# A decoder layer on one core: fourteen products of zeros leave TensorE's queue, and all five written orders are made anew

## What is computed

```python
x = x + attention(layernorm(x), Wqkv, Wo)        # 16 heads of 16, rotary positions, causal
x = x + cross_attention(layernorm(x), ctx, mask) # one head of 256, softmax over 256 context rows
x = x + ffn(layernorm(x), ...)                   # 8 experts of 176, the best 2 of each token, and a shared one of 352
```

## Time and profile before

| what | us |
|---|---|
| three runs | 269.67, 270.72, 271.45 |
| their median | 270.72 |
| span of the profiled execution | 271.7 |
| busy in it: PE, DVE, ACT, POOL | 259.4, 170.0, 174.8, 122.4 |
| mean granted TensorE clock | 0.994 |

### The profile page before, as it was taken

One profiled execution on the slowest core, in us unless ns is written; L12 is line 12 of the kernel. 1 busy time (PEld: TensorE's weight loads), 2 busy tenths in 40 slices (PEclk: granted clock), 3 DMA queues, 4 the chain that ended last, 5 costly groups with the idle time before them and its releaser, 6 DMA issues.

```text
span 271.7 us, 4900 instructions
## 1 busy us (share of the span) xinstructions
PE 259.4 (95%) x1805; PEld 210.2 (77%) x1810; DVE 170.0 (63%) x361; ACT 174.8 (64%) x292; POOL 122.4 (45%) x133
## 2 busy tenths in 40 slices
...
PEclk9997999999999999999999999999999999999999
...
DMA packets 11879, 17.08 MB, mean 63 GB/s; under 512 B 1904, under 2 KB 8272, under 8 KB 11856
## 3 DMA queue, kind: packets, MB, share of 16 engines
...
## 4 chain that ended last, share of the span: by engine, by line
PE 71%; POOL 8%; DMA 6%; DVE 6%; issue 4%; ACT 3%; SPq 2%; DVEq 0%; ACTq 0%
PE bank L789 26%; PE bank L898 13%; PE bank L802 11%; PE bank L951 4%; DMA res<-x 4%; POOL prob_lo L419 3%; DMA w_raw<-w 3%; PE bank L843 3%; PE bank L796 2%; PE bank L829 2%; PE bank L867 2%; PE bank L822 2%; PE bank L847 2%; POOL w_lo L426 1%; PE bank L824 1%
## 5 line engine op out<-in xcount | busy, mean ns | idle before, releaser
L419 POOL TENSOR_TENSOR prob_lo<-prob,prob_hi 128x1536 f16<-128x1536 f32 x16 | 49.9, 3120 | 14.9 <-ACT prob_hi L542 14.8
L789 PE MATMUL bank<-x_hi,w_hi 128*128 128x512 f32 x112 | 45.5, 406 | 0.0
L789 PE MATMUL bank<-x_hi,w_lo 128*128 128x512 f32 x112 | 44.2, 395 | 0.0
L789 PE MATMUL bank<-x_lo,w_hi 128*128 128x512 f32 x112 | 44.1, 393 | 0.0
L615 DVE TENSOR_REDUCE negm<-bank 128x2 f32<-128x512 f32 (+1 forms) x48 | 31.6, 685 | 8.6 <-PE bank L824 6.6
L771 DVE TENSOR_TENSOR h_lo<-h_c,h_hi 128x512 fp32r<-128x512 f32 x28 | 23.6, 845 | 21.0 <-ACT h_hi L581 20.8
L581 ACT CAST h_hi<-h_c 128x512 fp32r<-128x512 f32 x28 | 17.3, 617 | 24.6 <-DVE h_c L766 17.1
L757 DVE TENSOR_TENSOR h_c<-bank,h_s 128x512 f32<-128x512 f32 x28 | 19.3, 688 | 21.9 <-PE bank L789 18.3
L898 PE MATMUL bank<-w_hi,h_hi 128*128 128x256 f32 x112 | 32.9, 294 | 0.1
L575 ACT ACTIVATE h_s<-bank 128x512 f32<-128x512 f32 x28 | 16.7, 596 | 24.7 <-PE bank L789 24.7
L898 PE MATMUL bank<-w_hi,h_lo 128*128 128x256 f32 x112 | 31.6, 283 | 0.0
(11 more groups left out here) (128 smaller groups left out, 573.3 us busy)
## 6 DMA issues: line engine op xcount, KB each, us to landing
w_raw<-w SPq DMA_DIRECT2D x3, 1792.0 KB, 8.2
...
```

The lines of the kernel that those rows point to most:

```text
L419: eng.tensor_tensor(prob_lo[:, b % 2], prob[:, b % 2], prob_hi[:, b % 2], ALU.subtract)\
L789: ins = pe.matmul(dst, a(k), c(k), start=(k == 0 and i == 0), stop=(k == kt - 1 and i == 2))
```

## The change

PE's list loses its eight `early` and `late` entries (`early.4`, `.3`, `.1`, `.2`, `.1`, `.1` and twice `late.1`), 14 products of zeros in all, and the branches that issued them go. The sixteen ahead of the list stay. All five lists are written anew from the same steps. No step but those is added or dropped, and no instruction or wait inside a step is changed.

```diff
     "SP": """
-        ln1.0 mt.0 mt.1 mt.2 mt.3 mt.4 ct.0 mt.5 w3.0 ct.1 ro.0 ro.1 cb.0 ct.2 ct.3 y.0 cb.1 y.1
+        ln1.0 mt.0 mt.1 mt.2 mt.3 mt.4 ro.0 ro.1 ct.0 w3.0 mt.5 ct.1 cb.0 ct.2 ct.3 cb.1 y.0 y.1
     "POOL": """
-        ln1.0 ln1.1 qk.0 sh.0 qk.1 sh.1 qk.2 ln1.2 w12.0 qk.3 ln1.3 sh.2 w12.1 sh.3 qk.4 tr.7 h.0 h.1 sh.4 h.2 h.3
-        qk.5 sh.5 h.4 w12.2 ln2.0 w12.3 h.5 h.6 qk.6 sh.6 ln3.0 h.7 qk.7 w12.4 w12.5 sh.7 ln2.1 w12.6 h.8 w12.7 h.9
-        w12.8 h.10 ln3.1 h.11 h.12 h.13 w12.9 w3.0 ln2.2 w3.1 h.14 w3.2 w12.10 w3.3 w3.4 w12.11 ln3.2 h.15 w3.5
+        ln1.0 ln1.1 qk.0 sh.0 qk.1 sh.1 ln1.2 ln1.3 qk.2 sh.2 qk.3 w12.0 tr.7 w12.1 sh.3 qk.4 h.0 h.1 sh.4 h.2 h.3
+        qk.5 sh.5 h.4 w12.2 ln2.0 w12.3 w12.4 h.5 h.6 qk.6 ln3.0 sh.6 qk.7 h.7 sh.7 h.8 ln2.1 w12.5 h.9 h.10 w12.6
+        ln3.1 h.11 w12.7 h.12 w12.8 w3.0 h.13 w3.1 w12.9 ln2.2 h.14 w3.2 w12.10 w12.11 w3.3 ln3.2 h.15 w12.12 w3.4
...
     "ACT": """
-        ln1n.0 xt.0 ln1n.1 v.0 sh.0 xt.1 vm.0 tr.0 tr.1 sh.1 w12.0 w12.1 w12.2 tr.4 tr.5 ln1n.2 sh.2 v.1 w12.3 sh.3
-        xt.2 ln1n.3 mt.0 w12.4 mt.1 vm.1 tr.8 tr.9 s.0 s.1 tr.12 tr.13 s.2 s.3 h.0 w12.5 s.4 s.5 h.1 s.6 s.7 s.8
+        ln1n.0 xt.0 ln1n.1 v.0 sh.0 w12.0 xt.1 vm.0 tr.0 tr.1 sh.1 tr.4 tr.5 sh.2 w12.1 ln1n.2 sh.3 v.1 xt.2 w12.2
+        mt.0 ln1n.3 mt.1 vm.1 tr.8 tr.9 s.0 s.1 tr.12 tr.13 s.2 s.3 h.0 s.4 s.5 h.1 sh.4 s.6 w12.3 s.7 s.8 h.2 s.9
...
-        s.30 s.31 xs.1 s.32 pt.1 h.10 s.33 mt.4 s.34 s.35 h.11 s.36 ln3n.1 s.37 t3.1 s.38 mt.5 vm.3 s.39 s.40 lg.1
-        s.41 up.0 h.12 h.13 ct.1 up.1 w3.0 dn.0 ot.2 s.42 s.43 s.44 dn.1 s.45 w3.1 up.2 ln2n.2 s.46 t2.2 h.14 s.47
-        w12.10 xs.2 up.3 w3.2 pt.2 w3.3 w3.4 up.4 w3.5 dn.2 h.15 w12.11 dn.3 ln3n.2 w3.6 up.5 t3.2 dn.4 w3.7 dn.5
+        pt.1 w12.6 vm.3 s.33 mt.4 s.34 s.35 h.11 ln3n.1 s.36 s.37 t3.1 s.38 w12.7 mt.5 s.39 h.12 s.40 lg.1 s.41 up.0
+        ct.1 w12.8 w3.0 w3.1 h.13 ot.2 up.1 w3.2 dn.0 w12.9 w3.3 s.42 s.43 w12.10 ln2n.2 s.44 s.45 t2.2 s.46 s.47 h.14
+        dn.1 xs.2 up.2 pt.2 up.3 dn.2 w12.11 w3.4 up.4 ln3n.2 h.15 dn.3 up.5 w3.5 dn.4 w3.6 w3.7 t3.2 w12.12 up.6 w3.8
...
     "DVE": """
-        ln1.0 ln1.1 zero.0 qk.0 ln1.2 v.0 ln1.3 qk.1 vm.0 kt.2 kt.3 qk.2 m.0 m.1 m.2 kt.6 kt.7 m.3 qk.3 m.4 m.5 m.6
-        m.7 m.8 m.9 m.10 m.11 v.1 zero.1 vm.1 kt.10 kt.11 qk.4 kt.14 kt.15 m.12 m.13 m.14 m.15 m.16 m.17 m.18 m.19
+        ln1.0 ln1.1 zero.0 qk.0 zero.1 v.0 qk.1 ln1.2 ln1.3 vm.0 kt.2 kt.3 qk.2 m.0 m.1 m.2 kt.6 m.3 kt.7 qk.3 m.4 m.5
+        m.6 m.7 m.8 m.9 m.10 m.11 v.1 vm.1 kt.10 kt.11 qk.4 kt.14 kt.15 m.12 m.13 m.14 m.15 m.16 m.17 pv.0 m.18 m.19
...
-        ln3.1 m.44 m.45 pv.9 m.46 m.47 t3.1 pv.10 lg.1 rk.1 up.0 pv.11 vm.3 on.2 dn.0 up.1 pv.12 wo.2 ln2.2 dn.1
-        pv.13 xs.2 up.2 xc.2 up.3 dn.2 ro.2 ln3.2 dn.3 up.4 pv.14 up.5 dn.4 t3.2 up.6 dn.5 pv.15 lg.2 rk.2 up.7 on.3
+        m.44 m.45 m.46 m.47 t3.1 vm.3 pv.10 lg.1 rk.1 up.0 pv.11 on.2 up.1 wo.2 ln2.2 dn.0 xs.2 pv.12 dn.1 xc.2 pv.13
+        up.2 up.3 dn.2 ro.2 ln3.2 dn.3 up.4 up.5 pv.14 t3.2 dn.4 up.6 lg.2 dn.5 rk.2 up.7 pv.15 on.3 dn.6 up.8 wo.3
...
     "PE": """
-        xt.0 qk.0 v.0 qk.1 xt.1 early.4 tr.0 tr.1 qk.2 tr.2 tr.3 m.0 tr.4 tr.5 m.1 m.2 tr.6 m.3 tr.7 qk.3 m.4
-        m.5 v.1 m.6 m.7 xt.2 m.8 m.9 mt.0 m.10 m.11 early.3 mt.1 tr.8 tr.9 qk.4 tr.10 s.0 tr.11 s.1 tr.12 s.2
-        tr.13 s.3 early.1 tr.14 early.2 tr.15 s.4 early.1 m.12 m.13 s.5 m.14 m.15 s.6 m.16 s.7 m.17 m.18 s.8
-        m.19 s.9 m.20 pv.0 s.10 m.21 m.22 pv.1 m.23 s.11 early.1 mt.2 qk.5 tr.16 tr.17 s.12 pv.2 s.13 tr.18 s.14
+        xt.0 qk.0 v.0 qk.1 xt.1 tr.0 tr.1 qk.2 tr.2 tr.3 m.0 tr.4 m.1 tr.5 m.2 m.3 tr.6 tr.7 qk.3 m.4 m.5 v.1 m.6 m.7
+        xt.2 m.8 m.9 mt.0 m.10 m.11 mt.1 tr.8 tr.9 s.0 qk.4 tr.10 tr.11 s.1 tr.12 s.2 tr.13 s.3 tr.14 tr.15 s.4 s.5
+        m.12 m.13 s.6 m.14 m.15 s.7 m.16 m.17 pv.0 m.18 s.8 m.19 s.9 m.20 m.21 s.10 m.22 m.23 s.11 pv.1 mt.2 qk.5
...
-        s.29 late.1 tr.31 s.30 s.31 m.36 m.37 t2.1 m.38 xs.1 m.39 m.40 s.32 pv.8 m.41 pt.1 m.42 s.33 m.43 ro.1
-        mt.4 s.34 m.44 s.35 pv.9 m.45 s.36 s.37 m.46 m.47 pv.10 t3.1 s.38 mt.5 s.39 late.1 s.40 lg.1 s.41 up.0
-        s.42 pv.11 ct.1 up.1 ot.2 s.43 pv.12 wo.2 s.44 s.45 pv.13 s.46 up.2 s.47 dn.0 t2.2 dn.1 xs.2 up.3 pt.2
+        m.43 ro.1 mt.4 s.34 s.35 m.44 pv.9 m.45 s.36 pv.10 m.46 m.47 s.37 t3.1 s.38 s.39 mt.5 s.40 lg.1 s.41 up.0 s.42
+        pv.11 ct.1 s.43 up.1 ot.2 pv.12 wo.2 up.2 s.44 s.45 dn.0 t2.2 s.46 s.47 xs.2 up.3 pt.2 pv.13 dn.1 ro.2 up.4
...
@@
                 elif part == "dn":
                     down(b)
-                elif part == "early":
-
-                    idle_products(ps_tail, b)
-                elif part == "late":
-
-                    pe.wait_ge(s["rope_ok"], NT * B)
-                    idle_products(ps_qk, b)
```

More of the change, by code:

```diff
@@ L61 @@
-        w12.12 w3.6 ln2.3 w3.7 w3.8 w12.13 w3.9 w3.10 w3.11 w3.12 ln3.3 w3.13
+        ln1.0 ln1.1 qk.0 sh.0 qk.1 sh.1 ln1.2 ln1.3 qk.2 sh.2 qk.3 w12.0 tr.7 w12.1 sh.3 qk.4 h.0 h.1 sh.4 h.2 h.3
+        qk.5 sh.5 h.4 w12.2 ln2.0 w12.3 w12.4 h.5 h.6 qk.6 ln3.0 sh.6 qk.7 h.7 sh.7 h.8 ln2.1 w12.5 h.9 h.10 w12.6
+        ln3.1 h.11 w12.7 h.12 w12.8 w3.0 h.13 w3.1 w12.9 ln2.2 h.14 w3.2 w12.10 w12.11 w3.3 ln3.2 h.15 w12.12 w3.4
+        w3.5 ln2.3 w3.6 w12.13 w3.7 w3.8 w3.9 w3.10 ln3.3 w3.11 w3.12 w3.13
@@ L69 @@
-        s.30 s.31 xs.1 s.32 pt.1 h.10 s.33 mt.4 s.34 s.35 h.11 s.36 ln3n.1 s.37 t3.1 s.38 mt.5 vm.3 s.39 s.40 lg.1
-        s.41 up.0 h.12 h.13 ct.1 up.1 w3.0 dn.0 ot.2 s.42 s.43 s.44 dn.1 s.45 w3.1 up.2 ln2n.2 s.46 t2.2 h.14 s.47
-        w12.10 xs.2 up.3 w3.2 pt.2 w3.3 w3.4 up.4 w3.5 dn.2 h.15 w12.11 dn.3 ln3n.2 w3.6 up.5 t3.2 dn.4 w3.7 dn.5
-        up.6 lg.2 w3.8 up.7 w12.12 w3.9 w3.10 ct.2 dn.6 up.8 dn.7 ot.3 up.9 ln2n.3 dn.8 t2.3 up.10 w12.13 dn.9 xs.3
-        pt.3 dn.10 w3.11 w3.12 up.11 ln3n.3 w3.13 up.12 t3.3 up.13 dn.11 dn.12 lg.3 dn.13 up.14 up.15 dn.14 ct.3
@@ L74 @@
-        dn.15 up.16 dn.16 up.17 dn.17 up.18 dn.18 up.19 dn.19 up.20 dn.20 up.21 dn.21 up.22 up.23 dn.22 dn.23 up.24
-        dn.24 up.25 up.26 dn.25 up.27 dn.26 dn.27
+        ln1n.0 xt.0 ln1n.1 v.0 sh.0 w12.0 xt.1 vm.0 tr.0 tr.1 sh.1 tr.4 tr.5 sh.2 w12.1 ln1n.2 sh.3 v.1 xt.2 w12.2
+        mt.0 ln1n.3 mt.1 vm.1 tr.8 tr.9 s.0 s.1 tr.12 tr.13 s.2 s.3 h.0 s.4 s.5 h.1 sh.4 s.6 w12.3 s.7 s.8 h.2 s.9
+        s.10 s.11 mt.2 h.3 tr.16 s.12 s.13 tr.17 s.14 sh.5 h.4 v.2 ot.0 tr.20 s.15 tr.21 vm.2 s.16 s.17 h.5 s.18
@@ new lines @@
+        ln2n.0 w12.4 s.19 t2.0 s.20 w12.5 xt.3 h.6 xs.0 pt.0 s.21 s.22 sh.6 ln3n.0 s.23 mt.3 t3.0 h.7 tr.24 sh.7 lg.0
+        s.24 tr.25 s.25 s.26 s.27 ct.0 h.8 ot.1 tr.28 s.28 s.29 tr.29 s.30 v.3 s.31 ln2n.1 s.32 t2.1 h.9 h.10 xs.1
+        pt.1 w12.6 vm.3 s.33 mt.4 s.34 s.35 h.11 ln3n.1 s.36 s.37 t3.1 s.38 w12.7 mt.5 s.39 h.12 s.40 lg.1 s.41 up.0
+        ct.1 w12.8 w3.0 w3.1 h.13 ot.2 up.1 w3.2 dn.0 w12.9 w3.3 s.42 s.43 w12.10 ln2n.2 s.44 s.45 t2.2 s.46 s.47 h.14
+        dn.1 xs.2 up.2 pt.2 up.3 dn.2 w12.11 w3.4 up.4 ln3n.2 h.15 dn.3 up.5 w3.5 dn.4 w3.6 w3.7 t3.2 w12.12 up.6 w3.8
@@ L76 @@
+        w3.9 dn.5 lg.2 up.7 w3.10 w3.11 ct.2 up.8 ot.3 dn.6 w3.12 up.9 ln2n.3 w3.13 w12.13 dn.7 t2.3 up.10 dn.8 xs.3
+        dn.9 up.11 pt.3 dn.10 up.12 dn.11 ln3n.3 dn.12 t3.3 up.13 up.14 dn.13 dn.14 lg.3 up.15 up.16 ct.3 dn.15 up.17
+        dn.16 dn.17 up.18 up.19 dn.18 dn.19 up.20 up.21 up.22 dn.20 up.23 dn.21 dn.22 up.24 up.25 dn.23 up.26 dn.24
+        dn.25 up.27 dn.26 dn.27
     """,
     "DVE": """
-        ln1.0 ln1.1 zero.0 qk.0 ln1.2 v.0 ln1.3 qk.1 vm.0 kt.2 kt.3 qk.2 m.0 m.1 m.2 kt.6 kt.7 m.3 qk.3 m.4 m.5 m.6
@@ L79 @@
-        m.7 m.8 m.9 m.10 m.11 v.1 zero.1 vm.1 kt.10 kt.11 qk.4 kt.14 kt.15 m.12 m.13 m.14 m.15 m.16 m.17 m.18 m.19
-        m.20 pv.0 m.21 m.22 m.23 pv.1 qk.5 pv.2 kt.18 pv.3 on.0 kt.19 v.2 wo.0 kt.22 ln2.0 kt.23 vm.2 m.24 m.25 m.26
-        m.27 pv.4 m.28 xs.0 m.29 m.30 qk.6 m.31 pv.5 m.32 xc.0 ro.0 ln3.0 m.33 m.34 m.35 pv.6 qk.7 t3.0 pv.7 lg.0
-        rk.0 on.1 kt.26 kt.27 wo.1 ln2.1 kt.30 kt.31 m.36 m.37 v.3 m.38 xs.1 m.39 m.40 m.41 pv.8 m.42 m.43 xc.1 ro.1
-        ln3.1 m.44 m.45 pv.9 m.46 m.47 t3.1 pv.10 lg.1 rk.1 up.0 pv.11 vm.3 on.2 dn.0 up.1 pv.12 wo.2 ln2.2 dn.1
@@ L84 @@
-        pv.13 xs.2 up.2 xc.2 up.3 dn.2 ro.2 ln3.2 dn.3 up.4 pv.14 up.5 dn.4 t3.2 up.6 dn.5 pv.15 lg.2 rk.2 up.7 on.3
-        dn.6 dn.7 up.8 wo.3 ln2.3 dn.8 up.9 up.10 xs.3 dn.9 dn.10 xc.3 ro.3 ln3.3 up.11 t3.3 up.12 dn.11 dn.12 up.13
-        lg.3 rk.3 up.14 dn.13 dn.14 up.15 dn.15 y.0 up.16 dn.16 up.17 dn.17 up.18 dn.18 up.19 dn.19 up.20 dn.20
-        up.21 dn.21 up.22 dn.22 up.23 dn.23 up.24 dn.24 up.25 dn.25 up.26 up.27 dn.26 dn.27 y.1
+        ln1.0 ln1.1 zero.0 qk.0 zero.1 v.0 qk.1 ln1.2 ln1.3 vm.0 kt.2 kt.3 qk.2 m.0 m.1 m.2 kt.6 m.3 kt.7 qk.3 m.4 m.5
@@ new lines @@
+        m.6 m.7 m.8 m.9 m.10 m.11 v.1 vm.1 kt.10 kt.11 qk.4 kt.14 kt.15 m.12 m.13 m.14 m.15 m.16 m.17 pv.0 m.18 m.19
+        m.20 m.21 m.22 m.23 pv.1 qk.5 pv.2 kt.18 pv.3 on.0 kt.19 v.2 wo.0 kt.22 kt.23 ln2.0 m.24 vm.2 m.25 m.26 m.27
```

(8 more changed lines are left out.)

18 lines of the change are left out of this document (8 added, 10 removed).

## The result

| what | us |
|---|---|
| changed kernel, four runs | 274.88, 276.42, 276.62, 278.41 |
| their median | 276.52 |
| kernel before, four runs | 269.67, 269.74, 270.72, 271.45 |
| ratio to before | 1.020, interval 1.015 to 1.026 |
| span of the profiled execution, and its own time | 274.5, 276.42 |

The prediction said 268.9 and no more than 272.3. The loss is 6.3 us. The granted clock had a part in it: the mean clocks of the four changed executions are 0.992, 0.988, 0.986 and 0.998, and the last of them is the fastest, 274.88, which is still 5.2 us above the fastest of before. The profiled execution's own time lies 1.9 above its span; by that the profile of before, with its span of 271.7, belongs to an execution of some 273.6 us, longer than any of the runs beside it.

A forecast was written before the change was run, and what follows sets the result against it. PE was taken as the bound (busy 95% of the span, full from 62 to 91 and 138 to 268.2 us). From 270.72, 1.3 at the start and 0.5 at 110 to 146 us came off: 268.9, range 265.7 to 272.3.

The forecast's parts named there:

- From 146 us on PE is full.: Last stretch: PE has work throughout, so ACT's saved table loads gain nothing and the later `ct.3` is hidden.
- idle PE behind 146: Sign named beforehand that would show the forecast wrong: PE waiting in the stretch after 146 us; no size given.
- I take 1.3: Start, to 37 us: `zero.1` fills DVE's hole, `qk.1` ends sooner; gain 1.3 us, bounds 0 and 2.8.
- the 1.38 go: 110 to 146 us: PE's 1.38 us wait for DVE's sum, behind `dn.0`'s 3.54 us subtraction, was to vanish.
- The 0.4 us that were to come back at `t2.2` and `xs.2`: 110 to 146 us: 0.4 us was to return as shorter waits at these two steps, set against the 1.38 gained.
- The small transfer behind w3: 110 to 146 us: `mt.5`'s transfer lands behind the w3 load, delaying `s.42`; loss 0.5 us, bounds 0 and 1.3.
- The zeros at 0: PE's 14 dropped zero products lay in waits, so removing them gains 0; bounds 0 and 3.1 us.
- 37 to 110 us at 0: Nearly the same step order, single waits change hands: 0, between a loss of 1 and a gain of 1 us.
- The table loads and `ct.3` at nothing: From 146 us: ACT loses one pair of table loads (2 x 1.28 us), `ct.3` comes later; both at no effect.
- The clock falls in new places: Rival, chance 0.15: without zeros PE idles, new half-clock stretches cost up to 1.71 us each; two give 272.3, three 274.0.
- The full clock at the start: Rival, chance 0.30: the clock does not fall near 22.7 us, the start gains 2.8 us, time 267.4.

The follow-up runs named there:

- e3: Changed kernel with the 14 products of zeros put back at matching places in PE's list: median 276.93 us, ratio 1.023.
- e12: Kernel before with one ACT step moved, `dn.3` behind `ln3n.2`: median 274.23 us, ratio 1.012.
- e1: Kernel before, unchanged, run and profiled again: median 270.20 us, ratio 1.001; its profiled execution took 269.66 us.
- e4: Changed kernel with `dn.3` moved ahead of `ln3n.2` and `h.15` on ACT: median 274.73 us, ratio 1.013.
- e5: Changed kernel with POOL's subtraction of each `h` step issued as three smaller instructions: median 274.04 us, ratio 1.014.
- e8: Kernel before with SP issuing `ro.0 ro.1 ct.0 w3.0` ahead of `mt.5`: median 271.67 us, ratio 1.007.
- e6: Changed kernel with SP issuing the transfer of `mt.5` ahead of the w3 load: median 276.03 us, ratio 1.024.
- e2: Kernel before with only the 14 products of zeros taken out: median 270.01 us, ratio 1.000.

## Why the prediction was wrong

**The step that failed: "From 146 us on PE is full."** I took the fullness of that stretch for a property of the kernel. It was one of the old lists: ACT's `dn.3` stood ahead of `ln3n.2`, and so DVE had done it before POOL began `h.15`. I had counted ACT there by its share ("ACT is busy only 62 of 130 us") and had not walked the new list through it as I did for the start. In the share nothing is late; in the order `ln3n.2` waits 2.92 us for POOL and `dn.3` stands behind it. It cost 3.0 us of waiting (3.02 in e3, 3.13 in e12). In the profile shown a half stretch came with it: from the start of `up.4` to that of `up.6` it takes 14.3 us where e3 has 13.1, 1.2 us more. The prediction named "idle PE behind 146" as what would show it wrong, and that was it.

**"I take 1.3" for the start and "the 1.38 go".** Both mechanisms happened (`qk.1` at 16.6 as worked out, no row of 3.5 us at `dn.0`), and against e1's execution, which has neither loss, neither is a gain. The prediction set its sum against the profile's own span, 271.7, and took its 0.98 us above the median of the times for the whole difference. But the time of an execution is 1.8 to 1.9 us more than its span: the profiled one took some 273.6, about 3 us over the median. That was the sign that its half stretch and its 3.54 us row are not in every execution. What share of the 1.38 us belongs in the median of before stays open (e1). The 0.4 us that were to come back at `t2.2` and `xs.2` didn't, but 0.29 came at `dn.1`, whose subtraction met `h.14` on POOL and took 2.78 us. Counting from 269.7 with nothing for both would have given a forecast of about no change, still 2% off.

**The small transfer behind w3: right, mis-sized.** I took 0.5 of at most 1.3; it is 1.38 after, 1.57, 1.74 and 2.04 in e3, e4 and e5, and 0.9 in e8. The size was off because I left `s.42` due at 127.19 as in the late profile; it was due at 125.03 (126.41 - 1.38). w3 landed at 126.4 as worked out, but by luck: it was issued at 116.82 and not at 118.7, and took 9.6 us and not 7.74. Undoing it alone gains nothing (e6), as w3 then comes too late for ACT.

**Right.** The zeros at 0: e2 gives 1.000, with an interval of 0.4% each way. 37 to 110 us at 0: `up.0` moves by 0.1 us. The table loads and `ct.3` at nothing: PE is busy 106.83 of 106.89 us behind 164.23.

**The rivals.** "The clock falls in new places" had the side right, and gave 274.0 for three; the profile has one, for 1.2 us, and two more of the four executions have a clock low enough for two. At the full clock the loss is still 5.2 of the 6.3 us. The falls did become more frequent: a lower clock in 33 of 68 executions of the ten kernels with the new lists, against 14 of 88 of the kernel before. Its reason was the missing zeros, and taking those out alone (e2, 1 of 10) brings no more of them, while the new lists with the zeros (e3) have 3 of 4. The full clock at the start was seen, at 2.4 us less at `qk.3` than in the profile of before, and is what e1 has too.

**The sum, against e1's execution.** PE's last product group starts at 269.5 instead of 262.9, 6.6 us later: 3.00 at `dn.3`, 1.38 at `s.42`, 0.29 at `dn.1`, less 0.20 of a wait at `lg.2` that went, 1.2 by the clock, 0.1 at `up.0`: 5.8. Some 0.8 us I can't place; e3, without the half stretch, has 1.0 of that kind. They lie between `up.0` and `dn.3`: from the start of `dn.3` to that of `dn.27` e3 takes 107.25 us, and e1 107.82, in which `t3.2` (0.41) and the wait at `lg.2` (0.20) are contained.

**What stays open.** Why the clock falls in one execution and not in the next of the same kernel; why it falls more often with the new lists; whether the zeros make it rarer; how often `dn.0` is blocked in the kernel before; and the 0.8 us.
